# Small-head attentions of a two-layer decoder: the weighting of the preceding key tile ahead of a step's fourth score tile

## The chip, the core and the metric

The program runs on one core of a Trainium2 chip. The metric is the device time of one execution in microseconds; lower is better. The engines named below work side by side, each through its own list of instructions in order, and meet only by semaphores: TensorE (PE in the profile, its weight loads apart as PEld), VectorE (DVE), ScalarE (ACT), GpSimd (POOL) and SyncE (SP, which issues DMAs).

## What is computed

The reference is a decoder of two layers on x of shape 8 x 512 x 256 with a context of 8 x 1024 x 256. Layer 0 is a state-space block, a cross attention with 16 heads of depth 16 over the 1024 context rows, and a feed-forward block with quantised weights and low-rank additions. Layer 1 is a self attention with 16 heads of depth 16 over 512 rows, a second cross attention with heads of 64 and a ternary feed-forward block. The change touches the two attentions with heads of 16, which share one function. Each computes, per batch and head:

```
logits = einsum('bhqd,bhkd->bhqk', q, k) * depth ** -0.5
weights = softmax(logits, axis=-1)
out = einsum('bhqk,bhkd->bhqd', weights, v)      # then heads joined, @ wo.T + bo, added to x
```

## The kernel before

The kernel runs in phases with a barrier of all engines between them. `attention` (line 1616) is called twice: as phase "ca" (cross attention, 1024 keys, tiles `ca_...`, operands `cl_...`) and as phase "aa" (self attention, 512 keys, tiles `aa_...`, operands `al_...`).

**Units.** A unit is one batch with a group of four heads, 32 in all (UNITS = 8 batches x 4 groups). Within a unit the loop runs over key tiles `kt` of 128 keys: KT = 8 in ca, 4 in aa. Queries are always the 512 of the batch, in the free dimension.

**Stacked operands.** q and k are kept in parts stacked along the partitions, 48 rows for a head, plus one row that carries the negated row maximum (49 rows). Heads 0 and 2 of a group are on partitions 0 to 48, heads 1 and 3 on 64 to 112, so their matmuls use the lower or the upper half of TensorE's rows.

**Work of a step (one unit, one key tile) on TensorE.**
- `scores(unit, u, kt, h)` (1773 to 1776), for the four heads h: one matmul 49 x 128 keys x 512 queries into `s_ps`. There are three score banks (S_BANKS = 3), handed out in turn, so a tile waits until the exp of the tile three earlier is done (`p_done`), or, every second unit, until a transposed output was copied (`on_t_done`).
- `max_pair(j)` (1760 to 1771): two matmuls 48 x 128 queries x 512 keys, one on each half of the rows, into one of two slots of `m_ps`. VectorE reduces the pair (`reduce_pair`, 1909); a slot is free again when its reduction is done. These are the row maxima of a later unit: `pairs_of` (1648) puts two pairs in each step of ca (early, then late; in key tiles 0 and 2 early, then behind), and in aa one (late) and three (early, late, behind) by turns.
- `weigh(unit, u, kt)` (1778 to 1787): the exps of the key tile times the values, four heads side by side in the columns, all 128 rows, accumulated in `o_ps` over the key tiles. It waits for the exp of the fourth score tile of its key tile, and for key tile 0 also for the copy of the preceding unit's output (`ot_done`) and the values. A step issues the weighting of the step before it.
- `turn` (1789) in key tile 2: four transposes of the preceding unit's output; `turn_back` (1797) in key tile 3 of every second unit: four transposes into a score bank; `project` (1804) in key tile 0: four matmuls with the output weights. They stand between scores 1 and 2 and use slots of `m_ps` (turn, project) or a score bank (turn_back).

**ScalarE** (1876 on) takes an exp for each score tile in order (`weight`, 1871) into `pr`, which holds two key tiles; the first exp of a step waits for the weighting two steps back. In key tile 1 it first copies the preceding unit's output (1860). **VectorE** takes the pairs in order, the negation and transposition of a unit's maxima (1917, 1920), the reciprocals and products of the output (1926, 1930) and the addition to x (1937). **SyncE** moves the maxima into the stacked operands and loads the operands of later units. GpSimd prepares weights of the next phase.

The order on TensorE is written out by hand; one step is scores 0 and 1, early pair, transposes or projection, scores 2, late pair, scores 3, weighting of the preceding key tile, pair behind.

Of the kernel before, what the change touches and what calls it, by code (L numbers as in the profile page):

```python
# [1615 lines left out]
def attention(nc, io, g, semctx, tag, keys, loads, bo, bv, beside=None):  # L1616
# [22 lines left out]
    def after(unit, kt):  # L1639

        if kt == TURN and unit > 0:
            yield "turn", unit - 1
        if kt == BACK and unit > 0 and unit % 2 == 0:
            yield "back", unit // 2 - 1
        if kt == OUT and unit > GROUPS:
            yield "project", unit - GROUPS - 1

    def pairs_of(unit, kt):

        if unit == 0:  # L1650
            first = MP + FIRST + sum(PAIRS[:kt]) + sum(CATCH_UP[:kt])
            pairs = list(range(first, first + PAIRS[kt] + CATCH_UP[kt]))
            return pairs[0:1], pairs[1:2], pairs[2:]
        first = MP * (unit + 1) + AHEAD + sum(PAIRS[:kt])
        pairs = [j for j in range(first, first + PAIRS[kt]) if j < MP * UNITS]
        if PAIRS[kt] == 1:
            return [], pairs, []
        if PAIRS[kt] == 2 and kt in (OUT, TURN):
            return pairs[0:1], [], pairs[1:2]
        return pairs[0:1], pairs[1:2], pairs[2:]  # L1660
# [22 lines left out]
    with ExitStack() as ctx:  # L1683
# [31 lines left out]
        with nc.Block() as block:  # L1715
# [21 lines left out]
            def _(pe):  # L1737
                def score_bank(kind, n):

                    before, i = s_turns.before(kind, n)  # L1740
                    if before == "tile":
                        pe.wait_ge(p_done, i + 1)
                    elif before == "back":
                        pe.wait_ge(on_t_done, i + 1)
                    return s_ps[:, s_turns.bank(kind, n), :]
# [14 lines left out]
                def max_pair(j):  # L1760

                    unit, y = j // MP, j % MP
                    u, r, qt, half = unit % GROUPS, y // (NT * HALVES), y // HALVES % NT, y % HALVES
                    if y == 0:
                        pe.wait_ge(keys_loaded[u], KEY_LOADS * (unit // GROUPS + 1))
                    out = max_banks("max", j)
                    for i in range(2):
                        rows = slice(64 * i, 64 * i + STACK)
                        last = pe.matmul(out[:, i, :], qs[rows, u, r, qt:T:NT], ks[rows, u, r, half * T:(half + 1) * T],  # L1769
                                         start=True, stop=True)  # L1770
                    last.then_inc(m_ready, 1)

                def scores(unit, u, kt, h):
                    rows, r = slice(64 * (h % 2), 64 * (h % 2) + STACK + 1), h // 2
                    out = score_bank("tile", GH * (unit * KT + kt) + h)
                    pe.matmul(out, ks[rows, u, r, kt * P:(kt + 1) * P], qs[rows, u, r, :], start=True, stop=True).then_inc(s_ready, 1)  # L1776

                def weigh(unit, u, kt):

                    if kt == 0:  # L1780
                        pe.wait_ge(ot_done, unit)
                        pe.wait_ge(values_loaded[u], VALUE_LOADS * (unit // GROUPS + 1))
                    pe.wait_ge(p_done, GH * (unit * KT + kt + 1))
                    for h in range(GH):
                        last = pe.matmul(o_ps[32 * h:32 * h + 32, :], vs[:, u, kt, h, :], pr[:, 2 * (kt % 2) + h // 2, h % 2, :],  # L1785
                                         start=(kt == 0), stop=(kt == KT - 1))
                    last.then_inc(pv_done, 1)

                def turn(unit):

                    pe.wait_ge(ot_done, unit + 1)
                    out = max_banks("turn", unit)
                    for qt in range(NT):
                        last = pe.transpose(out[:, 0, qt * P:(qt + 1) * P], ot[:, qt * P:(qt + 1) * P], g.ident[:, :])
                    last.then_inc(turned, 1)

                def turn_back(pair):
                    pe.wait_ge(on_done, 2 * pair + 2)
                    out = score_bank("back", pair)
                    for qt in range(NT):  # L1800
                        last = pe.transpose(out[:, qt * P:(qt + 1) * P], on[:, qt, :], g.ident[:, :])
                    last.then_inc(back, 1)

                def project(n):
                    b, j = n // NT, n % NT
                    pe.wait_ge(on_t_done, KD * (b + 1))
                    out = max_banks("project", n)
                    for k in range(KD):
                        last = pe.matmul(out[:, 0, 0:D], on_t[:, b % 2, k, j * P:(j + 1) * P], w_o[:, k, :],
                                         start=(k == 0), stop=(k == KD - 1))  # L1810
                    last.then_inc(proj_ready, 1)
# [10 lines left out]
                for unit in range(UNITS):  # L1822
                    u = unit % GROUPS
                    pe.wait_ge(shift_done, 64 * (unit + 1))
                    for kt in range(KT):
                        early, late, behind = pairs_of(unit, kt)
                        scores(unit, u, kt, 0)
                        scores(unit, u, kt, 1)
                        for j in early:
                            max_pair(j)  # L1830
                        for kind, n in after(unit, kt):
                            if kind == "turn":
                                turn(n)
                            elif kind == "back":
                                turn_back(n)
                            else:
                                project(n)
                        scores(unit, u, kt, 2)
                        for j in late:
                            max_pair(j)  # L1840
                        scores(unit, u, kt, 3)
                        if kt > 0:
                            weigh(unit, u, kt - 1)
                        elif unit > 0:
                            weigh(unit - 1, (u - 1) % GROUPS, KT - 1)
                        for j in behind:
                            max_pair(j)
                weigh(UNITS - 1, GROUPS - 1, KT - 1)
# [1667 lines left out]
```

## Time and profile before

| | |
|---|---|
| runs (3) | 5183.59, 5193.1, 5194.74 us; median 5193.1 |
| span of the profiled execution | 5187.8 us (the page gives no other time for it; the span is 5.3 under the median) |
| mean granted clock of TensorE | 0.969 of full |
| TensorE busy | 4826.5 us, 93%, 23995 matmuls |
| weight loads | 2643.1 us, 51% |
| VectorE | 3645.6 us, 70% |
| ScalarE | 2944.7 us, 57% |
| GpSimd | 2639.4 us, 51% |
| DMA | 576.28 MB, 111 GB/s on average |
| phase ca, first to last score load | 987.5 to 1755.4 us |
| phase aa, first to last score load | 2104.4 to 2531.0 us |

The span runs from the first to the last instruction of one execution that the hardware profiler recorded. Busy shares are means over phases with different limits. The starts of instructions are recorded; the ends of matmuls are modelled, so a start is the safer number. In a timeline, instructions that follow each other in one group are merged (xN is their count), and the brackets give the idle time of the engine ahead of the group with what ended it.

### The profile page before, as it was taken

The page shows a single profiled execution, that of the slowest core. Times are in us where ns is not written, and L with a number is a line of the kernel's source. Part 1 is how long each engine was busy: PE and PEld are TensorE (multiplying, and loading weights), DVE is VectorE, ACT ScalarE, POOL GpSimd, SP SyncE. Part 2 cuts the span into 40 slices and gives each one's busy share as a digit, 9 for nine tenths or more (in the row PEclk, how much of TensorE's full clock was granted, in tenths as well). Part 3 has the DMA queues.
Part 4 walks back from the last instruction along what each step waited for, and adds up shares of the span by engine and source line. Part 5 has one row for each costly group of instructions (what it writes and reads, how often), then busy time and mean ns, then how long its engine had stood idle before and what let it go on. Part 6 is the DMA issues. An engine that isn't in the chain of part 4 may idle for free. (4 is left out here: it accounts for less than half of the span.)

```text
span 5187.8 us, 71148 instructions
## 1 busy us (share of the span) xinstructions
PE 4826.5 (93%) x23995; PEld 2643.1 (51%) x24010; DVE 3645.6 (70%) x6559; ACT 2944.7 (57%) x6256; POOL 2639.4 (51%) x1567
## 2 busy tenths in 40 slices
PE   6899997899999898899879999999999999999976
PEld 5555555344444487344445555555555555555533
DVE  8666666788888587788656666666676666666658
ACT  5677773477777654567534444444544444454457
POOL 5555554200000251530147878777787878777740
PEclk9999998799999999799989999999999999999989
DMA  6566667432222005432454333333334333343300
GB/s 219 194 232 239 232 231 237 133 88 71 74 74 69 12 1 184 124 92 82 155 142 98 80 95 88 88 90 85 96 80 98 86 90 90 86 97 78 90 17 29
DMA packets 344186, 576.28 MB, mean 111 GB/s; under 512 B 49120, under 2 KB 142368, under 8 KB 342800
## 3 DMA queue, kind: packets, MB, share of 16 engines
q1 hardware_dynamic: 341616, 567.53, 38.1%
q8 instruction: 193, 3.16, 0.3%
q10 hardware_dynamic: 2208, 4.20, 0.2%
q14 instruction: 169, 1.38, 0.1%
HBM read 335.54 MB, written 201.85 MB: 104 GB/s over the span
## 5 line engine op out<-in xcount | busy, mean ns | idle before, releaser
L3005 POOL TENSOR_TENSOR la_acc<-la_acc,la_pr 128x1024 f32<-128x1024 f32 x704 | 1696.6, 2410 | 491.9 <-ACT la_pr L2964 456.5
L2964 ACT ACTIVATE la_pr<-la_s_ps 128x512 f32<-128x512 f32 x1536 | 794.1, 603 | 972.4 <-PE la_s_ps L2813 970.3
L2820 PE MATMUL la_o_ps<-la_pr,lw_vf 128*64 128x512 f32 x3072 | 743.9, 605 | 0.0
L2812 PE MATMUL la_s_ps<-la_q_hl,lw_k_hh 128*128 128x512 f32 x1536 | 691.8, 450 | 1.8 <-ACT la_q_hs L2940 1.4
L1909 DVE TENSOR_REDUCE ca_mx<-ca_m_ps 128x2 f32<-128x1024 f32 x512 | 600.7, 1217 | 118.5 <-PE ca_m_ps L1769 118.5
L1871 ACT ACTIVATE ca_pr<-ca_s_ps 128x512 f32<-128x512 f32 x1024 | 542.0, 600 | 205.4 <-PE ca_s_ps L1776 202.1
L3026 DVE TENSOR_REDUCE la_mx<-la_m_ps 128x2 f32<-128x1024 f32 x384 | 462.9, 1205 | 212.0 <-PE la_m_ps L2795 203.8
L2813 PE MATMUL la_s_ps<-la_q_hs,lw_k_l 65*128 65x512 f32 x1536 | 608.3, 396 | 0.0
L3026 DVE TENSOR_REDUCE la_mx<-la_misc 128x2 f32<-128x1024 f32 x384 | 465.8, 1213 | 1.3 <-PE la_misc L2795 1.3
L2812 PEld LDWEIGHTS la_s_ps<-la_q_hl,lw_k_hh 128*128 128x128 f32 x1536 | 290.0, 189 | 243.2 <-ACT la_pr L2964 103.8
L2820 PEld LDWEIGHTS la_o_ps<-la_pr,lw_vf 128*64 128x64 f32 x3072 | 186.3, 136 | 346.4 <-issue 227.8
L1909 DVE TENSOR_REDUCE aa_mx<-aa_m_ps 128x2 f32<-128x1024 f32 x256 | 306.2, 1215 | 70.5 <-PE aa_m_ps L1769 67.3
L1871 ACT ACTIVATE aa_pr<-aa_s_ps 128x512 f32<-128x512 f32 x512 | 275.3, 602 | 121.7 <-PE aa_s_ps L1776 121.7
L1776 PE MATMUL ca_s_ps<-cl_qs,cl_ks 49*128 49x512 f32 x1024 | 324.9, 465 | 9.5 <-ACT ca_pr L1871 6.3
L2813 PEld LDWEIGHTS la_s_ps<-la_q_hs,lw_k_l 65*128 65x128 f32 x1536 | 292.3, 190 | 36.6
L3038 DVE RECIPROCAL la_rden<-la_den 128x128 f32<-128x128 f32 x256 | 241.1, 944 | 88.7 <-ACT la_den L2950 88.7
L2363 POOL MEMSET ff_zeros<- 128x4 f32 x1 | 0.1, 102 | 595.8 <-POOLq L3402 595.8
L3050 DVE TENSOR_TENSOR g_x<-g_x,la_misc 128x512 f32<-128x512 f32 x128 | 88.1, 688 | 302.0 <-PE la_misc L2839 302.0
L1769 PE MATMUL ca_m_ps<-cl_ks,cl_qs 48*128 48x512 f32 x1024 | 253.9, 492 | 41.2 <-DVE ca_mx L1909 35.3
L1785 PE MATMUL ca_o_ps<-ca_pr,cl_vs 128*32 128x512 f32 x2048 | 276.2, 612 | 0.0
L3021 DVE TENSOR_TENSOR la_q_hl<-la_misc,la_q_hl 64x512 fp32r<-64x512 f32 x128 | 88.1, 689 | 242.5 <-ACT la_q_hl L2930 240.4
L1776 PEld LDWEIGHTS ca_s_ps<-cl_qs,cl_ks 49*128 49x128 f32 x1024 | 135.5, 190 | 233.5 <-ACT ca_pr L1871 190.1
(414 smaller groups left out, 8980.3 us busy)
## 6 DMA issues: line engine op xcount, KB each, us to landing
lw_k_hh<-scratch_k_high SPq DMA_DIRECT2D x128, 512.0 KB, 6.5
scratch_k_high<-sc_k_high SPq DMA_DIRECT2D x128, 256.0 KB, 2.6
scratch_k_low<-sc_k_low SPq DMA_DIRECT2D x128, 256.0 KB, 2.8
lw_w_parts<-scratch_w_parts SPq DMA_DIRECT2D x64, 512.0 KB, 6.1
lw_k_l<-scratch_k_low SPq DMA_DIRECT2D x64, 512.0 KB, 8.4
lw_vf<-scratch_xv SPq DMA_DIRECT2D x64, 512.0 KB, 4.1
cl_ks<-scratch_k_rows SPq DMA_DIRECT2D x384, 64.0 KB, 2.8
scratch_vaug<-sc_v SPq DMA_DIRECT2D x16, 1024.0 KB, 4.4
```

Of the source, the lines that this page charges most:

```text
L1769: last = pe.matmul(out[:, i, :], qs[rows, u, r, qt:T:NT], ks[rows, u, r, half * T:(half + 1) * T], start=True, stop=True)
L1776: pe.matmul(out, ks[rows, u, r, kt * P:(kt + 1) * P], qs[rows, u, r, :], start=True, stop=True).then_inc(s_ready, 1)
L1785: last = pe.matmul(o_ps[32 * h:32 * h + 32, :], vs[:, u, kt, h, :], pr[:, 2 * (kt % 2) + h // 2, h % 2, :], start=(kt == 0), stop=(kt == K ...
L1871: act.activation(pr[:, 2 * (kt % 2) + h // 2, h % 2, :], s_ps[:, s_turns.bank("tile", n), :], ACT.Exp, scale=scale).then_inc(p_done, 1)
L1909: dve.tensor_reduce(mx[:, unit % 2, qt, r:GH:2, half], m_ps[:, m_turns.bank("max", j), :, :], AX.X, ALU.max).then_inc(m_reduced, 1)
L2812: pe.matmul(s_ps[:, bank, :], k_hh[:, par, h, keys], q_hl[:, par, h, :], start=True, stop=False)
L2813: pe.matmul(s_ps[:, bank, :], k_l1[:, par, h, keys], q_hs[:, par, h, :], start=False, stop=True).then_inc(s_ready, 1)
L2820: last = pe.matmul(o_ps[XD * h:XD * h + XD, :], vf[:, par, st, XD * h:XD * h + XD], pr[:, st % LAG, h, :], start=(st == 0), stop=(st == XT ...
L2964: act.activation(pr[:, st % LAG, h, :], s_ps[:, (2 * st + h) % 3, :], ACT.Exp, scale=scale).then_inc(p_done, 1)
L3005: pool.tensor_tensor(total, total, exps, ALU.add).then_inc(acc_done, 1)
L3026: dve.tensor_reduce(mx[:, qt, :, c], pair_banks(i)[:, :, :], AX.X, ALU.max).then_inc(m_reduced, 1)
L3038: dve.reciprocal(rden[:, part], den[:, part]).then_inc(rden_done, 1)
```

## The change

In each step the call that weighs the preceding key tile moves from behind `scores(unit, u, kt, 3)` to ahead of it; it now follows the late pairs. The pairs behind stay last, now directly behind scores 3. The order of the score banks and of the slots of `m_ps` is the same. ScalarE's, VectorE's, GpSimd's and SyncE's lists are the same.

```diff
                         scores(unit, u, kt, 2)
                         for j in late:
                             max_pair(j)
-                        scores(unit, u, kt, 3)
                         if kt > 0:
                             weigh(unit, u, kt - 1)
                         elif unit > 0:
                             weigh(unit - 1, (u - 1) % GROUPS, KT - 1)
+                        scores(unit, u, kt, 3)
                         for j in behind:
                             max_pair(j)
                 weigh(UNITS - 1, GROUPS - 1, KT - 1)
```

## Rows read from the trace of the kernel before

**Rows 1.** By stretch: length, busy time (count) per engine, clock, DMA share, GB/s.

```profile
1018.00:1755.00 737.00, 700.18 (x4207) 318.72 (x4205) 597.78 (x624) 545.55 (x1035) 11.01 (x12) 1.00 0.25 69
...
1805.00:1970.00 165.00, 159.41 (x1092) 144.85 (x1092) 140.44 (x361) 86.00 (x106) 84.25 (x76) 1.00 0.00 1
...
2136.00:2531.00 395.00, 382.08 (x2190) 175.79 (x2186) 316.73 (x375) 279.34 (x527) 90.69 (x67) 1.00 0.30 83
```

**Rows 2.** Groups of score weight loads: busy, mean | idle before, releaser.

```profile
L1776 PEld LDWEIGHTS ca_s_ps<-cl_qs,cl_ks 49*128 49x128 f32 x989 | 129.1, 188 | 224.2 <-ACT ca_pr L1871 186.2 <-issue 37.9
...
L1776 PEld LDWEIGHTS aa_s_ps<-al_qs,al_ks 49*128 49x128 f32 x482 | 69.2, 192 | 90.9 <-ACT aa_pr L1871 87.9 <-issue 1.8
```

**Rows 3.** Timeline, plain step: start, length, engine, line, operation, tiles, count, idle.

```profile
1325.01 0.19 PEld L1776 LDWEIGHTS ca_s_ps<-cl_qs,cl_ks 49*128 49x128 f32 x2 [0.84 <-ACT ca_pr L1871]
...
1325.35 0.81 PE L1769 MATMUL ca_m_ps<-cl_ks,cl_qs 48*128 48x512 f32 x3
...
1325.59 0.40 PE L1776 MATMUL ca_s_ps<-cl_qs,cl_ks 49*128 49x512 f32 x1
1325.60 2.06 ACT L1871 ACTIVATE ca_pr<-ca_s_ps 128x512 f32<-128x512 f32 x4 [0.60 <-PE ca_s_ps L1776]
...
1326.25 0.18 PEld L1776 LDWEIGHTS ca_s_ps<-cl_qs,cl_ks 49*128 49x128 f32 x1 [0.35 <-ACT ca_pr L1871]
...
1326.68 0.16 PEld L1785 LDWEIGHTS ca_o_ps<-ca_pr,cl_vs 128*32 128x32 f32 x8 [0.24 <-ACT ca_pr L1871]
...
1327.67 0.19 PEld L1776 LDWEIGHTS ca_s_ps<-cl_qs,cl_ks 49*128 49x128 f32 x2 [0.84 <-issue]
```

**Rows 4.** Timeline, weight loads, first attention, key tiles 0 and 1.

```profile
1303.70 0.19 PEld L1776 LDWEIGHTS ca_s_ps<-cl_qs,cl_ks 49*128 49x128 f32 x2 [0.84 <-issue]
...
1304.37 0.73 PEld L1809 LDWEIGHTS ca_m_ps<-cl_w_o,ca_on_t 128*128 128x128 f32 x4 [0.25 <-issue]
...
1305.43 0.19 PEld L1776 LDWEIGHTS ca_s_ps<-cl_qs,cl_ks 49*128 49x128 f32 x2 [0.33 <-ACT ca_pr L1871]
...
1306.86 0.31 PEld L1769 LDWEIGHTS ca_m_ps<-cl_ks,cl_qs 48*128 48x128 f32 x2 [0.84 <-issue]
...
1308.81 0.31 PEld L1769 LDWEIGHTS ca_m_ps<-cl_ks,cl_qs 48*128 48x128 f32 x2 [1.06 <-DVE ca_mx L1909]
...
1309.02 0.21 PEld L1776 LDWEIGHTS ca_s_ps<-cl_qs,cl_ks 49*128 49x128 f32 x1
...
1309.60 0.16 PEld L1785 LDWEIGHTS ca_o_ps<-ca_pr,cl_vs 128*32 128x32 f32 x8 [0.38 <-issue]
```

**Rows 5.** Timeline, weight loads, same unit, key tile 2 with transposes.

```profile
1310.60 0.19 PEld L1776 LDWEIGHTS ca_s_ps<-cl_qs,cl_ks 49*128 49x128 f32 x2 [0.84 <-ACT ca_pr L1871]
...
1311.26 0.42 PEld L1794 LDWEIGHTS ca_m_ps<-g_ident,ca_ot 128*128 128x128 f32 x4 [0.24 <-issue]
...
1311.85 0.19 PEld L1776 LDWEIGHTS ca_s_ps<-cl_qs,cl_ks 49*128 49x128 f32 x2 [0.17 <-ACT ca_pr L1871]
```

**Rows 6.** Timeline, VectorE then weight loads, second attention, unit's maxima.

```profile
2301.15 1.23 DVE L1909 TENSOR_REDUCE aa_mx<-aa_m_ps 128x2 f32<-128x1024 f32 x1 [0.64 <-PE aa_m_ps L1769]
...
2302.87 2.30 DVE L1909 TENSOR_REDUCE aa_mx<-aa_m_ps 128x2 f32<-128x1024 f32 x2
...
2305.23 0.31 PEld L1769 LDWEIGHTS aa_m_ps<-al_ks,al_qs 48*128 48x128 f32 x2 [0.29 <-DVE aa_mx L1909]
```

**Rows 7.** Timeline, weight loads, second attention, key tile 1 in three units.

```profile
2300.36 0.19 PEld L1776 LDWEIGHTS aa_s_ps<-al_qs,al_ks 49*128 49x128 f32 x2 [0.84 <-ACT aa_pr L1871]
...
2313.91 0.18 PEld L1776 LDWEIGHTS aa_s_ps<-al_qs,al_ks 49*128 49x128 f32 x2 [0.84 <-ACT aa_pr L1871]
...
2326.96 0.19 PEld L1776 LDWEIGHTS aa_s_ps<-al_qs,al_ks 49*128 49x128 f32 x2 [0.84 <-ACT aa_pr L1871]
```

**Rows 8.** By stretch as in rows 1: second attention, units 1, 2.

```profile
2121.70:2138.60 16.90, 16.90 (x70) 6.72 (x70) 10.44 (x12) 8.98 (x17) 16.49 (x8) 0.57 0.41 122
2138.60:2151.50 12.90, 12.28 (x74) 5.79 (x76) 10.90 (x13) 9.46 (x18) 11.95 (x13) 1.00 0.43 130
```

## Prediction

> **What bounds the kernel now.** The table of the page says that TensorE is busy for 93% of the span, but a busy share is no chain, and the chain of waits on the page only covers the last phase. So I read the two phases that the diff touches by themselves. Their steady parts are 737 and 395 us long, TensorE is busy for 95% and 97% of them, VectorE for about 80%, ScalarE for about 72%, with the granted clock at 1.00 [rows 1]. No engine but TensorE is near full, and what TensorE still waits for is named by the groups of instructions: before the weight loads of the score tiles (line 1776) it idles 186.2 us in the first attention and 87.9 us in the second until an exp of ScalarE (line 1871) is done [rows 2].
>
> Next, one plain step (a key tile with no transpose and no projection). The reader should follow the starts. Scores 0 and 1 are loaded at 1325.01, the matmul of the early maxima starts at 1325.35, that of scores 2 at 1325.59: one stream on the same half of the rows takes 0.24 us. The exps start at 1325.60, scores 3 are loaded only at 1326.25, the weighting at 1326.68, the next scores 0 at 1327.67 [rows 3]. The loop that sets the 2.66 us is: scores 0, its exp, scores 3 (there are three score banks, so tile n waits for the exp of tile n-3), the weighting, scores 0. Its terms are 1.24 us from one scores to the scores that waits for its exp, 0.43 from scores to weighting, 0.99 for the weighting. The late pair of maxima lies inside the 1.24 us and costs nothing now.
>
> **The change, part by part.** No instruction is added or removed, no DMA moves, and the queues of SP and GpSimd are as they were. 32 units with 8 key tiles each and 32 with 4 make 384 steps; one wait moves. The weighting asks for the exp of the preceding step's scores 3. Scores 2 of this step, ahead of it in both orders, ask for the same exp (n-3 again), so the moved wait itself is worth nothing. The weighting's own waits on the output copy, on the values and of ScalarE on the weighting come earlier or stay met. What moves is the place of scores 3: one weighting later, behind nothing but the head of the next step. So a new loop stands: scores 3, their exp, the next step's scores 2, late pair, weighting, scores 3.
>
> Plain step, afterwards: scores 3 are loaded where scores 0 now are, and by the same terms scores 2 of the next step follow 1.24 us later. Behind them stands the late pair, which shares the lower half of the rows with scores 2, one more stream of 0.24; then 0.43 to the weighting and 0.99 for it [rows 3]. Sum 1.24 + 0.24 + 0.43 + 0.99 = 2.90, against 2.66: **0.24 us more**. The wait for the exp of scores 0 which the weighting fills is 0.35 us by the idle of the weight load [rows 3]; it goes, and a wait of about 0.9 us ahead of scores 2 is late next: they now start 0.34 us after scores 0 (the early pair is in between), and then 1.24.
>
> The other steps of the first attention. Scores 3 and scores 1 are both on the upper half, so whatever follows the head of a step through both halves comes one stream (0.24) later. That cost is not in the trace of before: it is 0 if the halves run wholly apart, and one stream otherwise; I take the stream, since the nearest rows, matmuls on one half, are 0.24 apart. Key tile 0 holds a projection: 0.67 to it, 1.06 for it [rows 4], 0.24 for the fuller head, then 0.43 and 0.99: 3.39. Key tile 2 holds the transposes: 0.66, 0.24, 0.59 for them [rows 5], 0.43, 0.99: 2.91. Key tiles 1 and 3 hang on VectorE: the pair issued behind the weighting is loaded at 1306.86, and the late pair waits until it is reduced, at 1308.81, that is 1.95 later; the weighting comes 0.79 after that, with scores 3 in between [rows 4]. Afterwards the pair is second on the upper half (between nothing and one stream; I take the middle, 0.12), and scores 3 are gone from between (0.79 - 0.24 = 0.55): 1.95 + 0.12 + 0.55 + 0.99 = 3.61, measured from scores 3 to scores 3. A unit of eight: 3.39 + 3.61 + 2.91 + 3.61 + 4 x 2.90 = 25.12, against 23.97 now (from 1303.70 to 1327.67) [rows 3, 4]. That is 1.15 a unit, and over the 31 steps from unit to unit **36 us**.
>
> The second attention has a late pair in every key tile, and three reductions in every second one. Key tile 0: 3.39 + 0.24 = 3.63. Key tile 3: 2.90. Key tiles 1 and 2 together: the first reduction starts 0.79 after the scores (2300.36, then 2301.15) [rows 6, 7], with the fuller head 1.03; from it to the release of key tile 2's late pair VectorE takes 4.08 (2305.23) [rows 6]; then 0.55 and 0.99: 6.65. Sum 13.18, and 0.59 more for the transposes back in every second unit (as long as those of rows 5), against 13.05 and 13.55 now [rows 7]. So 0.13 and 0.22, mean 0.18; over 31, **6 us**. The first unit and the tail of each phase keep their parts.
>
> Sum: 42 to 43 us. The page gives 5187.8 us as span and no other time for the profiled execution; the median of the runs is 5.3 above it. With 43 on each, the span would be 5230.8 and the median 5236.1: **5236 us**. The bounds of this case: without the fuller heads (0.24 in key tiles 0 and 2 of 31 units of eight, in key tile 0 of 31 of four) it is 22 less, 5214; if each of the 384 steps loses another 0.06 because two score tiles start together, it is 23 more, 5259.
>
> **The rivals.** First, **faster**: the weighting fills the wait and scores 2 don't wait. This decides if the exp of scores 3 is done by the turn of the next scores 2, under 0.34 us after their load, where 1.24 is measured [rows 3]. A plain step would be the streams alone: 0.34, two of 0.24, 0.33 to the weighting (0.43 less the 0.10 of a load), 0.99, so 2.14; four a unit at 0.52 are 64 us, and key tile 3 of the second attention 16: 5113. Against it stand the three banks and an exp of 0.6 us. Chance 5%.
>
> Second, **no change**: the new loop stands, but the late pair runs while scores 2 wait, on halves that take work apart. Then 0.24 goes from each plain step and from key tiles 0 and 3 of the second attention: 30 and 15 us less, 5191. For it: matmuls of the two halves do overlap (three of line 1769 and one of 1776 between 1325.35 and 1326.16) [rows 3]. Against it: at key tile 1 the late pair waits until 1308.81 and scores 3 behind it are loaded at 1309.02, not before [rows 4]; nothing passes a waiting instruction there. The Trainium skill ("TensorE: Matmul & The Clock Gate", Part 3) says the same of matmuls, that they keep program order and only weight loads are pulled ahead; by that rule this case is excluded and the time is 5236, and where halves overlap in the trace nothing contradicts it for a waiting tile. Chance 8%.
>
> Third, **slower still**: TensorE, idle for about 0.9 us in each step, falls from 2.4 to 1.2 GHz for stretches. The price is in the second attention's start: unit 1 took 16.90 at a mean clock of 0.57, unit 2 took 12.90 at 1.00 [rows 8], so 4.0 us a unit. A tenth of 1180 us at that clock is about nine such units, 36 us: 5272. Against it: other stages held 1.00 with the engine at 97% and at 95% [rows 1], and here the same work spreads over 2.90 us in place of 2.66, 8% thinner. The skill's same page, Part 1, has the clock follow how busy the engine has lately been; the trace bears that out only as far as TensorE was at the lower clock behind the phases' starts, and shows no fall within the steady parts. Chance 5%.
>
> **How the numbers follow.** Forecast 82%, the others 5, 8 and 5. A measurement of this kernel can tell about 0.2%, 10 us, from no change. Faster by more is the first rival, 0.05; within it the second and a little of the first's lesser forms, 0.09; slower 0.86. The range takes in the forecast's bounds, 5214 to 5259, and a little beyond on either side, where an error in the reduction-bound tiles would lead: 5210 to 5262.
>
> **What the profile would show.** Right: in a plain step scores 3, 0 and 1 loaded together, scores 2 about 1.25 later with ScalarE as releaser, the weighting 0.67 behind them, steps of 2.90; units of 25.1 and about 13.2 and 13.8. The exps in two bunches, three and then one. Wrong: scores 2 at 0.34 to 0.6 (first rival), steps of 2.66 with the late pair's matmuls ahead of scores 2 (second), a granted clock under 1.00 between 1018 and 1755 us (third). A gain on TensorE's halves that I counted as a cost would show as projections still 0.67 behind scores 0.

## The result

The changed kernel took 5231.3 us (median of 4 runs, 5217.3 to 5265.1), the kernel before 5188.4 us in the same comparison (4 runs, 5183.6 to 5194.7): ratio 1.009, interval 1.0071 to 1.011. It is 43 us slower by the medians. A later and larger series, told below, has 5231.2 (6 runs) against 5194.7 (17 runs), ratio 1.0083, interval 1.0052 to 1.0114.

The profiled execution has a span of 5225.4 us, 37.6 more than before. The page shows the same number of instructions on each engine, and busy times within 27 us of before, so the loss is mostly waiting and not work (engine, busy us, share, count; then the granted clock in 40 slices of the span):

```profile
PE 4837.7 (93%) x23995; PEld 2669.9 (51%) x24010; DVE 3646.2 (70%) x6559; ACT 2931.5 (56%) x6256; POOL 2637.3 (50%) x1567
...
PEclk9899998899999899799989999999999999999989
```

Where it sits: the loads of the score tiles in each attention, from the view by tile (count; shortest/median/longest ns; first and last start). First attention:

```profile
L1776 PEld LDWEIGHTS ca_s_ps<-cl_qs,cl_ks x1024: 182/183/334, 992.4 to 1786.3; 49*128 49x128 f32 x171
```

Second attention:

```profile
L1776 PEld LDWEIGHTS aa_s_ps<-al_qs,al_ks x512: 182/183/334, 2137.4 to 2570.3; 49*128 49x128 f32 x171
```

That is 793.9 us against 767.9 (987.5 to 1755.4 before), and 432.9 against 426.5 (2104.4 to 2531.0 before): 26.0 and 6.4 us, together 32.4 of the 37.6. The first attention also started 4.9 us later, in phases whose code is the same.

These two differences are not all loop. From the starts of the units, the first unit of the first attention took 26.3 us against 30.2 before, where the lower clock lasted longer at its start (until 1010 us, now until 1001). Units 2 to 31 grew by 24.4 us together. The last unit grew by 5.5 us, mostly since the clock fell at 1776 us, before it ended. In the second attention the steady units make about 4 of the 6.4 us and the last unit 1.8.

One plain step, the counterpart of rows 3 (timeline: start, length, engine, line, operation, tiles, count, idle and releaser). Scores 3, 0 and 1 are now loaded together (x3 at 1360.84), the exp starts 0.53 later, scores 2 are loaded at 1362.01, held by an exp (TensorE's loads were idle for 0.53 us ahead of them), the weighting follows at 1362.68, the next three at 1363.67:

```profile
1360.84 0.29 PEld L1776 LDWEIGHTS ca_s_ps<-cl_qs,cl_ks 49*128 49x128 f32 x3 [0.84 <-ACT ca_pr L1871]
...
1361.37 2.06 ACT L1871 ACTIVATE ca_pr<-ca_s_ps 128x512 f32<-128x512 f32 x4 [0.78 <-PE ca_s_ps L1776]
...
1362.01 0.18 PEld L1776 LDWEIGHTS ca_s_ps<-cl_qs,cl_ks 49*128 49x128 f32 x1 [0.53 <-ACT ca_pr L1871]
...
1362.02 0.41 PEld L1769 LDWEIGHTS ca_m_ps<-cl_ks,cl_qs 48*128 48x128 f32 x2
...
1362.68 0.16 PEld L1785 LDWEIGHTS ca_o_ps<-ca_pr,cl_vs 128*32 128x32 f32 x8 [0.25 <-ACT ca_pr L1871]
...
1363.67 0.29 PEld L1776 LDWEIGHTS ca_s_ps<-cl_qs,cl_ks 49*128 49x128 f32 x3 [0.84 <-ACT ca_pr L1871]
```

The step shown is 1.17 + 0.67 + 0.99 = 2.83 us; the plain steps of units 9 to 28 have a median of 2.84, before of 2.66 to 2.67. The wait of the score loads for exps, counterpart of rows 2, rose in the first attention from 186.2 us (in a stretch of 737 us) to 290.1 (in one of 762):

```profile
L1776 PEld LDWEIGHTS ca_s_ps<-cl_qs,cl_ks 49*128 49x128 f32 x984 | 130.4, 186 | 310.3 <-ACT ca_pr L1871 290.1 <-issue 20.3
```

The tiles with a projection (key tile 0) and with a reduction ahead of the late pair (key tile 1), counterpart of rows 4. From scores 3 at 1363.67 the projection comes 0.90 later, scores 2 at 1365.63, the weighting at 1366.06, and the next scores 3 at 1367.05; key tile 1 then lasts until 1370.66, its late pair held by VectorE until 1369.11:

```profile
1363.67 0.29 PEld L1776 LDWEIGHTS ca_s_ps<-cl_qs,cl_ks 49*128 49x128 f32 x3 [0.84 <-ACT ca_pr L1871]
...
1364.57 0.73 PEld L1809 LDWEIGHTS ca_m_ps<-cl_w_o,ca_on_t 128*128 128x128 f32 x4 [0.25 <-issue]
1365.63 0.18 PEld L1776 LDWEIGHTS ca_s_ps<-cl_qs,cl_ks 49*128 49x128 f32 x1 [0.33 <-ACT ca_pr L1871]
1366.06 0.16 PEld L1785 LDWEIGHTS ca_o_ps<-ca_pr,cl_vs 128*32 128x32 f32 x8 [0.24 <-ACT ca_pr L1871]
1367.05 0.18 PEld L1776 LDWEIGHTS ca_s_ps<-cl_qs,cl_ks 49*128 49x128 f32 x1 [0.84 <-ACT ca_pr L1871]
...
1369.11 0.31 PEld L1769 LDWEIGHTS ca_m_ps<-cl_ks,cl_qs 48*128 48x128 f32 x2 [0.69 <-DVE ca_mx L1909]
1369.67 0.16 PEld L1785 LDWEIGHTS ca_o_ps<-ca_pr,cl_vs 128*32 128x32 f32 x8 [0.24 <-issue]
1370.66 0.29 PEld L1776 LDWEIGHTS ca_s_ps<-cl_qs,cl_ks 49*128 49x128 f32 x3 [0.84 <-ACT ca_pr L1871]
```

In the steady part of the first attention every unit now takes 24.85 us against 23.97. Read from scores 0 to scores 0, the four plain steps make about 0.7 of the 0.88 more. Key tiles 0 and 2 grew by 0.22 and 0.24, key tiles 1 and 3 shrank by 0.12 each.

### The profile page after: what moved, and what is told of

The parts are those of the page before. It is cut to its first block and busy times, and to the rows that moved or that the text cites. A ratio compares the mean times of both kernels' runs of the same rounds, so it can differ in the third digit from the quotient of the medians.

```text
span 5225.4 us, 71148 instructions
## 1 busy us (share of the span) xinstructions
PE 4837.7 (93%) x23995; PEld 2669.9 (51%) x24010; DVE 3646.2 (70%) x6559; ACT 2931.5 (56%) x6256; POOL 2637.3 (50%) x1567
## 3 DMA queue, kind: packets, MB, share of 16 engines
q1 hardware_dynamic: 341616, 567.53, 37.6%
q8 instruction: 193, 3.16, 0.3%
## 5 line engine op out<-in xcount | busy, mean ns | idle before, releaser
L2812 PEld LDWEIGHTS la_s_ps<-la_q_hl,lw_k_hh 128*128 128x128 f32 x1536 | 290.1, 189 | 243.3 <-ACT la_pr L2964 103.1
L1769 PE MATMUL ca_m_ps<-cl_ks,cl_qs 48*128 48x512 f32 x1024 | 333.1, 479 | 30.9 <-DVE ca_mx L1909 25.0
```

What stands on the lines that cost most here:

```text
L2812: pe.matmul(s_ps[:, bank, :], k_hh[:, par, h, keys], q_hl[:, par, h, :], start=True, stop=False)
```

## Experiments

Two theories stand against each other in most of them. The first is that of the prediction: with three score banks, scores 2 wait for the exp of the preceding scores 3, and the change makes a loop of scores 3, exp, scores 2, late pair, weighting. The other is that TensorE itself loses the time (three score tiles at the head of a stretch, fuller halves of the rows), or the clock.

### Which exp is in the loop: one exp taken twice

Four kernels take the exp of one score tile twice in each step, the first time into a spare tile that nothing reads; the result is unchanged. Here with h == 3, in the other pair h == 0:

```diff
+        spare = pool_.sb("spare", [P, T])
...
                     act.wait_ge(s_ready, n + 1)
+                    if h == 3:
+                        act.activation(spare[:, :], s_ps[:, s_turns.bank("tile", n), :], ACT.Exp, scale=scale)
                     act.activation(pr[:, 2 * (kt % 2) + h // 2, h % 2, :], ...
```

The fourth exp twice, in the kernel before:

> The kernel before, the exp of the fourth score tile taken twice in each step (the first time into a spare tile). It costs ScalarE 0.48 us more in each of 384 steps. Theory A (before, the exp of scores 3 is in no loop; ScalarE needs 5 x 0.49 = 2.4 of 2.66): plain steps stay 2.66 to 2.68, in all at most 5 us more. Rival C (either exp is as near to the loop as the other): steps of 3.1, some 100 us more.

The fourth exp twice, in the changed kernel:

> The changed kernel, the exp of the fourth score tile taken twice in each step. Theory A (the exp of scores 3 is in the loop of every plain step): plain steps 2.84 to 3.33 us, units of eight 24.86 to about 27.0, in all about 100 us more than the changed kernel, some 5330. Rival D (the added time of the change is TensorE's own: three score tiles at the head of a stretch, fuller halves; ScalarE has 0.8 us to spare in each step): steps stay 2.84 to 2.9, at most 20 us more.

The first exp twice, in the kernel before:

> The kernel before, the exp of the first score tile taken twice in each step: 0.48 us of ScalarE more, as in the run with the fourth. Theory A (before, this exp is in the loop): plain steps 2.66 to 3.15 us, units of eight 26.5, about 109 us more, 5295 to 5305. Rival F (which exp is lengthened doesn't matter before, ScalarE has 0.6 us to spare in a step): as the run with the fourth exp twice, 2.67 and 5182.

The first exp twice, in the changed kernel:

> The changed kernel, the exp of the first score tile taken twice. Theory A (it is in no loop now): plain steps stay 2.84, units of eight 24.9, some 5 us more in the second attention; 5225 to 5245. Rival F (ScalarE's total work in the step is what counts after the change): 0.48 more in each plain step, as the run with the fourth exp twice, some 5325.

Measured, one run each, with the plain step and the mean steady unit of the first attention from the score loads of its trace:

| | kernel before | changed kernel |
|---|---|---|
| as it is | 5188.4; 2.66; 23.97 | 5231.3; 2.84; 24.85 |
| fourth exp twice | 5182.0; 2.67; 23.98 | 5323.8; 3.33; 27.18 |
| first exp twice | 5314.7; 3.16; 26.55 | 5269.1; 2.85; 25.05 |

The four totals were expected at most 5193, 5330, at most 5305 and at most 5245. In a plain step the same 0.49 us of ScalarE is free in one cell of each row and costs its whole length in the other. (With the first exp twice in the changed kernel, units still grew by 0.2, in key tiles 0 and 3.) The timeline of a plain step in the kernel before with the fourth exp doubled shows the extra exp at 1344.25, and the next scores 0 still 2.67 behind the last:

```profile
1342.20 0.18 PEld L1777 LDWEIGHTS ca_s_ps<-cl_qs,cl_ks 49*128 49x128 f32 x2 [0.84 <-issue]
...
1343.45 0.18 PEld L1777 LDWEIGHTS ca_s_ps<-cl_qs,cl_ks 49*128 49x128 f32 x1 [0.37 <-ACT ca_pr L1874]
...
1343.88 0.16 PEld L1786 LDWEIGHTS ca_o_ps<-ca_pr,cl_vs 128*32 128x32 f32 x8 [0.25 <-ACT ca_pr L1874]
...
1344.25 0.62 ACT L1873 ACTIVATE ca_spare<-ca_s_ps 128x512 f32<-128x512 f32 x1
...
1344.87 0.19 PEld L1777 LDWEIGHTS ca_s_ps<-cl_qs,cl_ks 49*128 49x128 f32 x2 [0.84 <-ACT ca_pr L1874]
```

In the changed kernel the same extra exp stands at 1380.74, directly behind scores 3, and scores 2 come only 1.66 behind them (1.17 without it), the next three 3.33 behind:

```profile
1380.21 0.29 PEld L1777 LDWEIGHTS ca_s_ps<-cl_qs,cl_ks 49*128 49x128 f32 x3 [0.84 <-ACT ca_pr L1874]
...
1380.74 0.60 ACT L1873 ACTIVATE ca_spare<-ca_s_ps 128x512 f32<-128x512 f32 x1 [0.93 <-PE ca_s_ps L1777]
...
1381.23 2.06 ACT L1874 ACTIVATE ca_pr<-ca_s_ps 128x512 f32<-128x512 f32 x4
1381.87 0.18 PEld L1777 LDWEIGHTS ca_s_ps<-cl_qs,cl_ks 49*128 49x128 f32 x1 [1.02 <-ACT ca_pr L1874]
...
1382.54 0.16 PEld L1786 LDWEIGHTS ca_o_ps<-ca_pr,cl_vs 128*32 128x32 f32 x8 [0.25 <-ACT ca_pr L1874]
...
1383.54 0.29 PEld L1777 LDWEIGHTS ca_s_ps<-cl_qs,cl_ks 49*128 49x128 f32 x3 [0.84 <-ACT ca_pr L1874]
```

So the change moved the loop of the plain steps from the first exp to the fourth. That ScalarE has time to spare in a step protects nothing. Two totals came out over their expectation: 5314.7 in place of at most 5305, and 5269.1 in place of at most 5245. The second did so outside the steady part, where the plain steps are as expected and the units within 0.15; it is taken up under the clock below.

### The size of the exp's term: two waits on one instruction

The prediction had 1.24 us from scores 3 to scores 2; 1.17 was measured. The exp that was in the loop before starts 0.59 behind its load (1325.01 and 1325.60 in rows 3), that of the loop after 0.53. The former is the first of its step and waits for two semaphores, the score tile and the weighting two steps back. Two kernels put the wait for the score tile first:

```diff
                     n = GH * (unit * KT + kt) + h
-                    act.wait_ge(s_ready, n + 1)
+                    if h > 0:
+                        act.wait_ge(s_ready, n + 1)
...
+                        act.wait_ge(s_ready, GH * (unit * KT + kt) + 1)
                         if unit * KT + kt > 1:
 
                             act.wait_ge(pv_done, unit * KT + kt - 1)
                         weight(unit, kt, 0)
```

In the kernel before:

> The kernel before; on ScalarE the wait for the score tile is put ahead of the wait for the weighting two steps back, for the first exp of each step. In both traces an exp with one wait starts 0.53 us behind its scores' load, the first exp of a step, with two waits, 0.60. Theory A (the wait that is met last must be the one on the instruction, else 0.07 is added, and in the kernel before that exp is in the loop): plain steps 2.66 to 2.60 us, units of eight 23.97 to 23.7, in all 8 to 11 us less, about 5178. Rival B (the first exp of a step is late for another reason, such as ScalarE having been idle): the exp still starts 0.60 behind, steps stay 2.66, 5188.

In the changed kernel:

> The changed kernel with the same swap of the two waits. Theory A (the loop of the changed kernel runs scores 3, exp, scores 2, late pair, weighting, and the first exp of a step is not in it): plain steps stay 2.84 us although the wait pair is gone, units 24.86, total as the changed kernel, 5225 to 5235. Rival C (the loop still runs over scores 0 and their exp): steps fall by 0.07 to 2.77, 17 us less in the first attention.

Measured: 5178.6 us (12 runs) against 5191.0 (17 runs), ratio 0.9976, interval 0.9967 to 0.9986; and 5217.0 in one run for the changed kernel with the swap. The plain step of the first fell to 2.61, the exp 0.54 behind the load:

```profile
1336.21 0.19 PEld L1776 LDWEIGHTS ca_s_ps<-cl_qs,cl_ks 49*128 49x128 f32 x2 [0.84 <-ACT ca_pr L1872]
...
1336.75 2.07 ACT L1872 ACTIVATE ca_pr<-ca_s_ps 128x512 f32<-128x512 f32 x4 [0.55 <-PE ca_s_ps L1776]
...
1337.40 0.18 PEld L1776 LDWEIGHTS ca_s_ps<-cl_qs,cl_ks 49*128 49x128 f32 x1 [0.30 <-ACT ca_pr L1872]
...
1337.83 0.16 PEld L1785 LDWEIGHTS ca_o_ps<-ca_pr,cl_vs 128*32 128x32 f32 x8 [0.25 <-ACT ca_pr L1872]
...
1338.83 0.19 PEld L1776 LDWEIGHTS ca_s_ps<-cl_qs,cl_ks 49*128 49x128 f32 x2 [0.84 <-ACT ca_pr L1872]
```

The changed kernel kept its step of 2.84 and its unit of 24.86, and its score loads of the first attention span 793.8 us (988.9 to 1782.7), against 793.9: the swapped exp is in no loop there. Its total was expected at 5225 to 5235; it lies at the low end of the changed kernel's runs and shows nothing else. The trace has the reason for the 0.06: in the kernel before, the wait for the score tile is a semaphore instruction of its own, at 1325.54, and the exp, which carries the wait for the weighting, starts 0.06 behind it. With the swap the separate wait, for the weighting, is over at 1336.35, and the exp carries the wait for the score tile. A pair of waits thus costs about 0.06 us if the one met last is not on the instruction itself, and the other order of the waits is worth 0.24% here.

### The late pair's term

> The changed kernel with the late pair of maxima put ahead of scores 2, where TensorE waits for the exp of scores 3. Theory A (the late pair sits in the loop behind scores 2): in the plain steps of the first attention it is hidden, 2.84 to about 2.61 us, less than the 2.66 of before. But the pair then waits for its reduction ahead of scores 2 and not behind it, so key tiles 1 and 3 grow by about 0.24, one plain step in two or three too, and the second attention, which is bound by the reductions in key tile 2, takes 9 us more; in all 5225 to 5240, no better than the changed kernel. Rival E (the late pair is hidden anyway and the added time is the place of scores 3): plain steps stay at 2.84.

```diff
+                        for j in late:
+                            max_pair(j)
                         scores(unit, u, kt, 2)
-                        for j in late:
-                            max_pair(j)
                         if kt > 0:
                             weigh(unit, u, kt - 1)
```

Measured: 5243.4 us in one run, where 5225 to 5240 was expected. The plain step fell to 2.60 (the weight loads of one step; the late pair is now in the x4 ahead of the wait):

```profile
1353.90 0.29 PEld L1776 LDWEIGHTS ca_s_ps<-cl_qs,cl_ks 49*128 49x128 f32 x3 [0.84 <-ACT ca_pr L1871]
1354.01 0.77 PEld L1769 LDWEIGHTS ca_m_ps<-cl_ks,cl_qs 48*128 48x128 f32 x4
1355.09 0.18 PEld L1776 LDWEIGHTS ca_s_ps<-cl_qs,cl_ks 49*128 49x128 f32 x1 [0.30 <-ACT ca_pr L1871]
1355.51 0.16 PEld L1785 LDWEIGHTS ca_o_ps<-ca_pr,cl_vs 128*32 128x32 f32 x8 [0.24 <-issue]
1356.50 0.19 PEld L1776 LDWEIGHTS ca_s_ps<-cl_qs,cl_ks 49*128 49x128 f32 x2 [0.84 <-ACT ca_pr L1871]
```

So the late pair costs 0.24 a step behind scores 2, as the sum had it, and the pair does not run ahead of a waiting tile by itself. From scores 0 to scores 0, key tiles 1 and 3 grew to 3.62 (from 3.39) and key tile 6 took 2.80. An undisturbed unit of the first attention took 24.55 against 24.85, some 9 us less in 31, and the second attention grew from 432.9 to 444.4 us, where 9 more were expected. What the plain steps gain, the steps that wait for a reduction lose.

Much of the rest of this total is the clock. The first attention took 802.8 us against 793.9 although its undisturbed units are shorter, since the granted clock fell several times within its steady part, here at 1518 and 1528 us (a stretch of 18 us at a mean of 0.62):

```profile
1518.00:1536.00 18.00, 17.16 (x77) 6.91 (x76) 10.65 (x13) 8.81 (x17) 0.00 (x0) 0.62 0.05 19
```

### The weighting one place further ahead

> The changed kernel with the weighting one place further ahead, in front of the late pair as well, still behind scores 2. Theory A (what counts is how much lies between the exp of scores 3 and the next scores 3): the late pair and scores 3 now stand behind the weighting, the loop holds the same parts and one more start of a stretch: plain steps 2.84 to about 2.94, the tiles bound by reductions lose more, since the late pair comes a weighting later; first attention 20 us, second 29 us over the changed kernel, about 5280. Rival G (weighting earlier is good in itself, it frees the exps' tile sooner): not above the changed kernel.

```diff
                         scores(unit, u, kt, 2)
-                        for j in late:
-                            max_pair(j)
                         if kt > 0:
                             weigh(unit, u, kt - 1)
                         elif unit > 0:
                             weigh(unit - 1, (u - 1) % GROUPS, KT - 1)
+                        for j in late:
+                            max_pair(j)
                         scores(unit, u, kt, 3)
```

Measured: 5282.1 us in one run, plain steps of 2.96 (2.94 expected), first attention 26 us and second 33 us over the changed kernel (20 and 29 expected). The weighting is no gain for coming early: what counts is the length of the loop it lies in.

### Only the plain tiles

> The order of the change in key tiles 4 to 7 of the first attention only, the order of before everywhere else. If each plain step simply cost 0.18 us more, four of them would make 0.7 a unit, 22 us in all (theory J, cost per step). Theory A (the cost is in a loop that closes only from one changed step to the next): three of the four steps show 2.84, and the first, where the loop of before is left and the weighting comes a stretch earlier, falls to about 2.15; key tile 0 behind them grows by 0.23. Units 24.1 to 24.15, 5 to 6 us in all, about 5194.

The order is "as changed" for kt >= 4 and "as before" otherwise, which in the second attention is always before. Measured: 5191.4 us (10 runs) against 5194.7 (17 runs), ratio 1.0004, interval 0.9992 to 1.0016. The totals can't tell the expected 5 us from nothing, but they exclude the 22 us of a cost per step. The steps of key tiles 4 to 7, read off the score loads of a unit (the x2, then the three x3, then the next unit's):

```profile
1343.19 0.19 PEld L1776 LDWEIGHTS ca_s_ps<-cl_qs,cl_ks 49*128 49x128 f32 x2 [0.84 <-issue]
...
1345.32 0.29 PEld L1776 LDWEIGHTS ca_s_ps<-cl_qs,cl_ks 49*128 49x128 f32 x3 [0.84 <-ACT ca_pr L1870]
...
1346.50 0.18 PEld L1776 LDWEIGHTS ca_s_ps<-cl_qs,cl_ks 49*128 49x128 f32 x1 [0.54 <-ACT ca_pr L1870]
...
1348.17 0.29 PEld L1776 LDWEIGHTS ca_s_ps<-cl_qs,cl_ks 49*128 49x128 f32 x3 [0.84 <-ACT ca_pr L1870]
...
1351.00 0.29 PEld L1776 LDWEIGHTS ca_s_ps<-cl_qs,cl_ks 49*128 49x128 f32 x3 [0.84 <-ACT ca_pr L1870]
...
1353.85 0.29 PEld L1776 LDWEIGHTS ca_s_ps<-cl_qs,cl_ks 49*128 49x128 f32 x3 [0.84 <-ACT ca_pr L1870]
```

They are 2.13, 2.85, 2.83 and 2.85 us; key tile 0 behind them takes 3.58 in place of 3.37, and a unit 24.19, which is 0.22 more than before. A cost per step would have given four times 0.18. The first step is the gain that one would hope for from the change: there the weighting does fill the wait for the exp of scores 0, and nothing has to wait for a late scores 3 yet. The next step pays for it, since scores 3 came later. It is a loan within the loop.

### An order for each loop

Both kernels have the swapped waits. The first has one order for each attention:

> The kernel before with the two waits of the first exp swapped, and the step's order chosen by what each loop leaves idle: first attention scores 0, early, scores 1, transposes or projection, scores 2, late, scores 3, behind, weighting; second scores 0, early, scores 1, transposes or projection, scores 2, scores 3, late, weighting, behind. Theory A (the loops add up from the terms of the traces): units of eight 22.95 us against 23.97, units of four 12.7 against 13.3, about 42 us less than before, 5148. Rival H (the swapped waits are all that helps, order in the other tiles is hidden): about 5179.

The second has one for each key tile:

> As the order by phase, with an order of its own for each key tile: in key tile 1 the pair behind or the late pair goes with scores 3 behind the weighting, in key tile 2 the weighting stands ahead of scores 2 (first attention) or ahead of the transposes (second), and key tile 3 of the second has the changed kernel's order. Theory A: units of eight 22.5 us, of four 12.1, about 75 us less than before, 5115. So the move of the weighting is worth something where it fills a wait for a reduction, and only there. Rival H: no better than the order by phase, since every step has one loop with the same parts; 5148.

In the table of the orders 0 to 3 stand for the scores, e, l and b for the early, late and behind pairs, a for transposes and projection, w for the weighting:

```diff
+                        order = {8: ("0e1a2l3bw", "0e1a2lwb3", "01ealw2b3") + ("0e1a2l3bw",) * 5,
+                                 4: ("0e1a23lwb", "0e1a2lw3b", "01ewa23lb", "0e1a2lw3b")}[KT][kt]
+                        for part in order:
...
```

Measured: 5153.9 us (5 runs), ratio 0.9934 (0.9921 to 0.9948), and 5130.4 us (4 runs), ratio 0.989 (0.9876 to 0.9903), against 5187.5 (9 runs). The expectations were 5148 and 5115: the direction, and 34 of 42 and 57 of 75 us of the size. The ranges of the two do not overlap, so the second gains 23.5 us over the first. Its units of eight take 22.73 and 22.99 us by turns, mean 22.86, where 22.5 was expected, those of four 12.14 and 12.52, mean 12.33, where 12.1 was. Which term of those sums was too low stays open. The plain steps are 2.61 as in the kernel with the swap alone, so all the rest comes from the other tiles. Key tile 1 of the first attention shows it: 2.14 us where before took 3.52. Of this, 0.82 came already with the first of the two kernels (2.70), in which the pair behind of key tile 0 is issued ahead of that tile's weighting; the weighting ahead of scores 3 then fills the wait for the exp and brings the other 0.56. Key tile 2, with the weighting ahead of scores 2, gains 0.57 between the two (3.61 to 3.04). Key tile 3 pays part of it back: it takes 3.77 and 3.50 by turns, where the first kernel took 3.16 and 2.61.

```profile
1314.35 0.18 PEld L1776 LDWEIGHTS ca_s_ps<-cl_qs,cl_ks 49*128 49x128 f32 x1 [0.84 <-ACT ca_pr L1872]
...
1315.49 0.16 PEld L1785 LDWEIGHTS ca_o_ps<-ca_pr,cl_vs 128*32 128x32 f32 x8 [0.25 <-issue]
1316.49 0.30 PEld L1776 LDWEIGHTS ca_s_ps<-cl_qs,cl_ks 49*128 49x128 f32 x3 [0.84 <-ACT ca_pr L1872]
```

So the moved weighting is worth something in single tiles that wait for a reduction (0.38 a unit of eight between these two kernels), and costs in a run of plain ones. In the second attention several places changed at once, and the weighting's share is not separated.

### How much of the 43 us is the loops

> The changed kernel once more, for the size of the effect. The score loads of the two phases, first to last, took 32 us more than before, the median of its four runs 43 us more, and the four lie 48 us apart with mean clocks of 0.970 to 0.959. Theory K (the loops cost 32 us, the rest is how long TensorE's lower clock lasted at a phase's start in single executions): many executions, most at a clock of 0.966 to 0.971, 30 to 40 us more than before, some up to 75 more at the lower clocks. Rival L (the loops cost more than the one profile showed): 43 us more with a narrow spread.

Measured: 5218.4, 5220.7, 5229.4, 5233.0, 5260.6 and 5273.5 us, at mean granted clocks of 0.971, 0.971, 0.969, 0.968, 0.960 and 0.956. The first series had 5217.3 at 0.970, 5227.2 at 0.968, 5235.4 at 0.966 and 5265.1 at 0.959. The kernel before lies between 5180.8 and 5199.9 in the 17 runs beside it. The fair comparison is at the same clock. At 0.970 and 0.971 the changed kernel has a median of 5218.4 (3 runs), the kernel before one of 5186.8 (15 runs of all its series); at 0.968 and 0.969 it is 5229.4 (3) against 5193.5 (19). That is 32 and 36 us, which agrees with the 32 us between the score loads. The profiled execution of this series is one of the long ones (5258.8 us of span). Its stretches, first at the start of the first attention, then in the second (length, busy times of PE, PEld, DVE, ACT, POOL, clock, DMA share, GB/s):

```profile
988.00:1081.00 93.00, 91.40 (x330) 34.53 (x329) 53.11 (x52) 43.08 (x82) 18.58 (x8) 0.50 0.27 69
1081.00:1800.00 719.00, 673.83 (x3976) 320.90 (x3976) 568.67 (x594) 505.03 (x974) 11.01 (x12) 1.00 0.24 67
...
2167.00:2194.00 27.00, 22.33 (x132) 9.61 (x129) 22.64 (x26) 17.11 (x33) 26.59 (x12) 1.00 0.51 143
2194.00:2239.00 45.00, 45.00 (x166) 16.83 (x164) 25.22 (x29) 20.77 (x39) 39.95 (x40) 0.51 0.28 81
```

TensorE stayed at the lower clock for 93 us, although it was busy for 98% of them; in the kernel before the first attention was at full clock from 1018 us on [rows 1], and in the first profiled execution of the changed kernel the stretch from 1009 to 1787 us had a mean of 0.99. The first three units took 105.0 us here and 74.5 there, the steady ones 24.87 and 24.85. In the second attention the clock rose at 2167 us and fell again from 2194 to 2239. Score load to score load, the two attentions took 26.8 and 9.7 us more than in the first profiled execution of the same kernel. The changed kernel with the first exp twice shows the same at its start, and a fall in its last two units:

```profile
987.00:1081.00 94.00, 92.67 (x332) 35.01 (x333) 53.32 (x52) 52.65 (x102) 18.60 (x8) 0.50 0.27 68
1081.00:1788.00 707.00, 666.71 (x3892) 310.51 (x3893) 569.65 (x590) 601.36 (x1176) 11.00 (x12) 1.00 0.25 68
1788.00:1828.00 40.00, 38.19 (x124) 10.76 (x116) 1.10 (x3) 24.57 (x48) 0.00 (x0) 0.50 0.00 1
```

That is the 5269 left over above.

## Why the prediction was right, and where it was off

**Direction and total.** Forecast 5236 us, measured 5231.3, within the range of 5210 to 5262; as a difference, 43 forecast and 43 measured. That equality is partly luck. The 5236 stood on a median of 5193.1 before, which is 5188.4 in this comparison. The terms of the loops were too high by about 10 us, and two of the four runs had a low clock (0.959 and 0.966), which the sum had at nothing. The larger series has 36.5 us between the medians, and at equal clocks it is 32 to 36.

**The new loop.** Right, and for the plain steps shown rather than argued: the doubled exps separate it from any cost in TensorE. In key tiles 0 and 2 the added 0.22 and 0.24 are those of the fuller head, as forecast; the fourth exp taken twice leaves key tile 0 as it is (3.37 us).

**The plain step.** 2.90 forecast, 2.84 measured. The mis-sized term is the 1.24 from scores 3 to scores 2, which measured 1.17. I took it from an exp with two waits and applied it to an exp with one. Four plain steps in 31 units make 7 us; the unit came to 24.85 in place of 25.12, 8 us for the first attention. Of the 36 us forecast there another 2 are missing since units 2 to 5 hold no projection and grew by 0.60. The prediction's wait of "about 0.9 us" ahead of scores 2 is how much later they start than before; the loads' idle time there is 0.53 us.

**The other tiles.** From scores 3 to scores 3, forecast and measured: key tile 0 3.39 and 3.38, key tiles 1 and 3 3.61 and 3.60, key tile 2 2.91 and 2.90. The fuller head, bounded between nothing and one stream, is the stream: the projection comes 0.90 behind the head where it was 0.67.

**The ends of the phases.** The prediction let the first unit and the tail of each phase keep their parts. The last unit of the second attention grew by 1.8 us (11.3 against 9.5), and that of the first by 1.5 where the clock held (21.7 against 20.2, the former in the later profiled execution).

**The exps.** Forecast in two bunches, three and one. They come as one run of four in 2.06 us, behind 0.78 us of idle time (1361.37 above): the fourth is ready before the third has ended. It changes no term.

**The second attention.** 6 us forecast, 6.4 measured, again partly luck. Its steady units grew by 0.06 and 0.21 (13.09 and 13.74 against 13.03 and 13.53) where 0.13 and 0.22 stood, which makes 4 us; the last unit made up for it.

**The wait that is filled.** The prediction held that it is filled and paid back by the wait ahead of scores 2. The kernel with only the plain tiles changed shows both halves: 2.13 in the first changed step, then 2.85.

**The rivals.** Faster: excluded by the step of 2.84. No change, by a late pair that runs during the wait: excluded, since moving the pair by hand gave the 0.24 that would have been there already. The program order of matmuls, which the prediction set against this rival, does not hold between the two halves in these traces: of a late pair in the changed kernel, the matmul of the upper half, second in the program and the one that signals, started at 1359.18 and that of the lower half at 1359.51, while scores 2 held the lower half from 1359.17. What held is that nothing passed the waiting scores 2. Slower still, by the clock: this had a chance of 5%, and in a weaker form it is there. Three of the ten executions of the changed kernel took 5261 to 5273 us at clocks of 0.956 to 0.960. The place was in part wrong: I looked for falls within the steady parts. In the later profiled execution most of the loss is that the rise at the start of the first attention came later, and one fall came in the second attention (2194 us); the kernel with the late pair ahead had falls within the steady part. The reason given, TensorE idle for about 0.9 us a step, is not shown: a step's loads were idle for 0.53 us, and TensorE was busy for 98% of the 93 us at the lower clock. What decides it, and whether the order has a part in it, is open; no run here held the clock apart from the order. The kernel before has no run under 0.966 among the 44 that stood beside the experiments, which speaks for a part of the order but doesn't show its way.

## What to carry to other kernels

Filling a wait of the busiest engine with work that is ready does nothing by itself. Write down the loop through the banks before and after, term by term, with what it delays: here a tile whose exp the next step needs was pushed behind the filler. To see which of several equal instructions is in a loop, take each one twice in a kernel of its own; the length of the step answers with the exp's whole length or with nothing. And try an order of its own for each kind of step, if the steps wait for different engines.

## What the runs showed of the hardware

- An instruction with two waits of which the last to be met is not its own starts about 0.06 us later (0.59 against 0.54 behind the score load); exchanging the two waits is worth 12 us in this kernel.
- Matmuls of the lower and the upper half of the rows overlap, and one can start ahead of an earlier one on the other half (1359.18 against 1359.51), but none passed a waiting instruction: scores 3 were loaded at 1309.02, behind a pair held until 1308.81 [rows 4], and the late pair at 1362.02 above, behind scores 2 held until 1362.01. Put ahead of scores 2, that pair ran during the wait.
- In two executions of the same changed kernel, TensorE's lower clock held at the start of the first attention until 1081 us in one and was all but over by 1009 in the other. TensorE was busy for 98% of the long stretch. The clock also fell again after it had risen: from 2194 to 2239 us, behind 27 us at full clock in which TensorE was busy for 83%. Three of ten runs had a mean clock of 0.956 to 0.960 and were 28 to 56 us longer than those at 0.968 to 0.971.
